# Causal self-attention scores of a transformer layer: three fp32r products of upper and lower halves in place of one fp32 product, and the output tile in another buffer's place

## What is computed

```python
    y = layernorm(x)                                   # (8, 512, 256)
    # attention(y, y, y, causal=True)
    scores = jnp.einsum('bqd,bkd->bqk', Q, K) / jnp.sqrt(d_k)
    scores = jnp.where(mask, scores, -inf)
    w = softmax(scores)
    sa = jnp.einsum('bqk,bkd->bqd', w, V)
    y = layernorm(y + sa)
```

## Time and profile before

| | |
|---|---|
| median of 3 runs | 622.27 us (617.64 to 622.56) |
| the profiled execution | 616.4 us, span 614.5 us |
| PE busy | 565.8 us, 92% of the span |
| DVE busy | 493.4 us, 80% |
| ACT busy | 378.4 us, 62% |
| POOL busy | 382.6 us, 62% |
| chain that ended last | PE 76%, issue 7%, POOL 6%, DVE 5%, ACT 4% |
| mean granted TensorE clock | 0.975 of full |

### The profile page before, as it was taken

The page is one execution under the profiler, slowest core; times in us unless marked ns, Lnnn a source line. Parts: engine busy times, 40 slices in busy tenths (PEclk is TensorE's granted clock), DMA queues, the critical chain, the costliest instruction groups (busy, mean ns, idle before and its releaser), DMA issues.

```text
span 614.5 us, 12404 instructions
## 1 busy us (share of the span) xinstructions
PE 565.8 (92%) x4021; PEld 537.4 (87%) x4021; DVE 493.4 (80%) x1220; ACT 378.4 (62%) x781; POOL 382.6 (62%) x466
## 2 busy tenths in 40 slices
PE   4776869999999999999999999999999999999765
PEld 3665868999999999999999999999999999989665
DVE  3688877888888888888888888887988878787762
ACT  3547465675748676667758575766666774746331
POOL 2554774676666766676657657675767656765621
PEclk9978979999999999999999999999999999999897
DMA  7700101010100101010101001010101010000000
GB/s 221 237 2 0 36 2 43 1 53 1 43 19 2 53 1 61 0 51 0 60 0 51 0 25 35 0 51 0 60 2 35 1 36 2 18 2 18 1 18 17
DMA packets 18742, 19.30 MB, mean 31 GB/s; under 512 B 1536, under 2 KB 18192, under 8 KB 18704
## 3 DMA queue, kind: packets, MB, share of 16 engines
q1 hardware_dynamic: 18704, 18.82, 10.0%
HBM read 14.62 MB, written 4.19 MB: 31 GB/s over the span
## 4 chain that ended last, share of the span: by engine, by line
PE 76%; issue 7%; POOL 6%; DVE 5%; ACT 4%; DMA 1%; SPq 1%; POOLq 0%; DVEq 0%; ACTq 0%
PE R L938 6%; PE R L940 5%; PE R L939 5%; PE TR L824 5%; PE O L986 5%; PE R L1004 4%; PE O L1049 4%; PE R L1006 4%; PE R L1005 4%; PE O L1051 4%; PE O L1050 4%; PE R L824 4%; PE O L1028 3%; PE O L1030 3%; PE O L1029 3%
## 5 line engine op out<-in xcount | busy, mean ns | idle before, releaser
L938 PE MATMUL R<-gu_hi,xqT_hi 128*128 128x352 f32 x256 | 85.4, 334 | 3.9 <-issue 3.0
L457 POOL TENSOR_TENSOR rs<-mv,neg_half 128x1 f32<-128x1 f32 (+1 forms) x112 | 69.2, 627 | 31.4 <-DVE mv L1277 30.1
L690 ACT ACTIVATE hqT_hi<-R 128x768 fp32r<-128x768 f32 x32 | 26.0, 813 | 98.8 <-PE R L824 98.8
L1004 PE MATMUL R<-y2T_hi,w_hi 128*128 128x256 f32 x256 | 77.3, 302 | 6.4 <-ACT e_full L717 3.4
L940 PE MATMUL R<-gu_hi,xqT_lo 128*128 128x352 f32 x256 | 82.4, 322 | 0.0
L939 PE MATMUL R<-gu_lo,xqT_hi 128*128 128x352 f32 x256 | 82.4, 322 | 0.0
L463 POOL TENSOR_TENSOR hs<-hh,h_rec 128x704 f32<-128x704 f32 x32 | 44.6, 1392 | 50.7 <-DVE h_rec L1313 50.7
L1049 PE MATMUL O<-w_hi,hT_hi 128*128 128x256 f32 x256 | 74.6, 291 | 0.0
L1006 PE MATMUL R<-y2T_hi,w_lo 128*128 128x256 f32 x256 | 73.1, 286 | 0.0
L1005 PE MATMUL R<-y2T_lo,w_hi 128*128 128x256 f32 x256 | 73.1, 285 | 0.0
L1051 PE MATMUL O<-w_hi,hT_lo 128*128 128x256 f32 x256 | 71.8, 281 | 0.0
(11 more groups left out here) (148 smaller groups left out, 1820.2 us busy)
## 6 DMA issues: line engine op xcount, KB each, us to landing
x_in<-in_x SPq DMA_DIRECT2D x16, 256.0 KB, 2.8
x_res<-in_x SPq DMA_DIRECT2D x16, 256.0 KB, 2.8
out<-x SPq DMA_DIRECT2D x32, 128.0 KB, 1.9
ctx_rows<-in_ctx SPq DMA_DIRECT2D x16, 64.0 KB, 2.5
hT<-in_L_xattn_w SPq DMA_DIRECT2D x1, 1024.0 KB, 8.0
hh<-in_L_xattn_w SPq DMA_DIRECT2D x1, 768.0 KB, 7.9
wd_raw<-in_L_ffn_w_down SPq DMA_DIRECT2D x1, 704.0 KB, 8.7
w_raw<-in_L_ffn_w_gate SPq DMA_DIRECT2D x1, 640.0 KB, 4.5
```

Source lines behind the costliest of these rows:

```text
L938: mm(o, xh, gu_hi[:, c, m, cols], start=(c == 0), stop=False)
L1004: mm(o, w1_hi[:, c, cols], y2T_hi[:, c, :], start=(c == 0), stop=False)
```

## The change

Three things change. `copy_y0T` on ACT writes the same copy as fp32r into `y0T_hi`. A new DVE instruction, `y0T_lower`, writes the bank minus `y0T_hi` into `y0T_lo`; it stands in DVE's slot after `hT_lower(b, g, 1)` and ahead of the place "self". Each fp32 product of the scores becomes three fp32r products, and the scores wait for `y0T_lo_set` as well as for `y0T_hi_set`. To make room, `x2` becomes numbers 512 to 1023 of each partition of `wd_raw`; its reads and writes stay as they were.

```diff
-        y0T = sb("y0T", [P, KC, S])
+        y0T_hi = sb("y0T_hi", [P, KC, S], F32R)
+        y0T_lo = sb("y0T_lo", [P, KC, S], F32R)
...
-        x2 = sb("x2", [P, T, D])
+        x2 = late_d(1)
...
-                act.activation(y0T[:, :, ROWS * h:ROWS * (h + 1)],
-                               TR[1][:].rearrange("p (c r) -> p c r", c=KC), ACT.Copy).then_inc(y0T_set, 1)
+                act.activation(y0T_hi[:, :, ROWS * h:ROWS * (h + 1)],
+                               TR[1][:].rearrange("p (c r) -> p c r", c=KC), ACT.Copy).then_inc(y0T_hi_set, 1)
...
+            def y0T_products(o, c, k, q, width):
+                keys, queries = slice(k, k + P), slice(q, q + width)
+                mm(o, y0T_hi[:, c, keys], y0T_hi[:, c, queries], start=(c == 0), stop=False)
+                mm(o, y0T_hi[:, c, keys], y0T_lo[:, c, queries], start=False, stop=False)
+                return mm(o, y0T_lo[:, c, keys], y0T_hi[:, c, queries], start=False, stop=(c == KC - 1))
+
             def scores(b, h):
-                wait(pe, y0T_set, b, h, 0, 1, 1)
+                wait(pe, y0T_hi_set, b, h, 0, 1, 1)
+                wait(pe, y0T_lo_set, b, h, 0, 1, 1)
...
-                    mm(bank(DIAG)[:, P:2 * P], y0T[:, c, q0 + P:q0 + ROWS], y0T[:, c, q0 + P:q0 + ROWS],
-                       start=(c == 0), stop=(c == KC - 1))
+                    y0T_products(bank(DIAG)[:, P:2 * P], c, q0 + P, q0 + P, P)
...
+            def y0T_lower(b, h):
+                wait(dve, y0T_hi_set, b, h, 0, 1, 1)
+                cols = slice(ROWS * h, ROWS * (h + 1))
+                v.tensor_tensor(y0T_lo[:, :, cols], TR[1][:].rearrange("p (c r) -> p c r", c=KC),
+                                f32(y0T_hi[:, :, cols]), ALU.subtract).then_inc(y0T_lo_set, 1)
...
                 if q1:
                     hT_lower(b, g, 1)
+                if live(b, h, 0):
+                    y0T_lower(b, h)
                 prepare(b, h, "self")
```

More of the change, by code:

```diff
@@ L211, in layer_program @@
         ln_out = [sem(f"ln_out{i}") for i in range(5)]
-        y0_turned, y0T_set = sem("y0_turned"), sem("y0T_set")
+        y0_turned, y0T_hi_set, y0T_lo_set = sem("y0_turned"), sem("y0T_hi_set"), sem("y0T_lo_set")
         scores_full, scores_diag = sem("scores_full"), sem("scores_diag")
@@ L955, in scores @@
                 for c in range(KC):
-                    mm(bank(DIAG)[:, P:2 * P], y0T[:, c, q0 + P:q0 + ROWS], y0T[:, c, q0 + P:q0 + ROWS],
-                       start=(c == 0), stop=(c == KC - 1))
+                    y0T_products(bank(DIAG)[:, P:2 * P], c, q0 + P, q0 + P, P)
                 for c in range(KC):
-                    last = mm(bank(DIAG)[:, 2 * P:4 * P], y0T[:, c, q0:q0 + P], y0T[:, c, q0:q0 + ROWS],
-                              start=(c == 0), stop=(c == KC - 1))
+                    last = y0T_products(bank(DIAG)[:, 2 * P:4 * P], c, q0, q0, ROWS)
                 last.then_inc(scores_diag, 1)
@@ L964, in scores @@
                         for c in range(KC):
-                            last = mm(bank(FULL)[:, ROWS * key:ROWS * (key + 1)], y0T[:, c, P * key:P * (key + 1)],
-                                      y0T[:, c, q0:q0 + ROWS], start=(c == 0), stop=(c == KC - 1))
+                            last = y0T_products(bank(FULL)[:, ROWS * key:ROWS * (key + 1)], c, P * key, q0, ROWS)
                     last.then_inc(scores_full, 1)
```

## The result

The changed kernel takes 627.65 us (median of 4 runs, 625.05 to 628.81) against 620.54 for the kernel before (median of 4, 617.64 to 622.56): a ratio of 1.0123, 95% interval 1.0079 to 1.0168, so some 7.6 us more (7.1 by the medians). That it is slower is clear of the noise; that it is slower by more than the 1% that the prediction named is not, since the interval begins at 0.79%. The profiled execution took 628.48 us, with a span of 626.5.

The account below looks back on a forecast made before the run. The prediction took PE to bound the steady part, with waits for other engines in slots 0 to 3. Steady +2.4 and start +4.4 gave +6.8 us, 629.1 on the 622.27 median; range 622 to 642 for 8 in 10.

Parts of the forecast that it names:

- the steady part: Slots 4 to 15: +0.30 us for each h = 0 slot, +0.10 for each h = 1, together +2.4 us.
- The price of a short fp32r product, p = 0.112: Scores on PE: a 128-column fp32r product takes 0.112 us, three 0.336 against 0.224 before; chance 0.42.
- The rival by fp32's price: Scores on PE: short fp32r products cost 0.224 us each; total +18.8 us, 641 us; chance 0.28.
- the one by columns: Scores on PE: short fp32r products cost 0.062 us each, by columns; total +1.6 us, 623.9 us; chance 0.12.
- The wait, 0.23 and 0.34: Steady slots: PE's first scores product ends later, waiting for DVE's lower part, by 0.23 us (h = 0) and 0.34 (h = 1).
- The products behind it, +0.07 and -0.24: Steady slots, scores after the first product: 1.27 us against 1.20 for h = 0, 2.68 against 2.93 for h = 1.
- What was costed at nothing: DVE's 0.68 us a slot, fitting into a 0.77 wait; the copy's new type; x2's home: no cost.
- The start, +4.4: Slots 0 to 3: DVE's order delays the scores; 3.2 + 1.0 + 0.2 = +4.4 us.
- Slot 0: Start: the lower part stands behind both find steps, so the scores end at 14.9 instead of 11.73: +3.2 us.
- the terms for slots 2 and 3: Start: slot 2 delays ff1 by 1.0 us, uncovered; slot 3 loses 0.2 us after cover.
- Slot 3's +0.2: Slot 3: scores end 2.8 us later, but PE's wait for e_full, with ACT behind, covers 2.6, leaving +0.2 us.
- The rival that the clock stays up in slot 3: Slot 3: PE's wait is cut in two, the clock doesn't fall, 2.3 us less; +4.5, 626.8 us; chance 0.10.

Follow-up runs that it names:

- e8: The changed kernel with each 128-wide product of the scores cut into two of 64 columns; one profile, span 638.3 us against the changed kernel's 626.5.
- e1: The changed kernel with its lower part and wait kept, but each scores product one fp32 product of the upper part; 1.0104 of the time before.
- e2: The changed kernel without the lower part and its wait, all three products upper part by upper part; 0.9927 of the time before.
- e5: The changed kernel with the first 6 of 18 products of down, tile 1, moved ahead of the scores on PE; 1.0039 of the time before.
- e7: e6 with the 128-wide scores product plain fp32 again from slot 4 on, from an added ACT copy; 1.0003 of the time before.
- e4: The kernel before with only x2 moved into the raw w_down's place; 0.9987 of the time before.
- e3: The changed kernel with the lower part at other places in DVE's order in slots 0 to 3; 1.0045 of the time before.
- e12: The changed kernel, unchanged, run once for a third profile; span 622.5 us.
- e10: The changed kernel, unchanged, run once for a second profile; span 627.6 us.
- e6: The changed kernel with both repairs, e3's DVE order in the first four slots and e5's split of down; 0.9994 of the time before.

## Why the prediction was right, point by point

The forecast was 629.1 us, or +6.8; the median is 627.65, and the ratio gives +7.6. The mean spans say the same: 617.5 for the four profiles of before's program and of x2's move, 625.5 for the three of the change, +8.0, made of +6.1 in the start, +3.2 in slots 4 to 15 and -1.2 in what follows, where the clock falls too at places that vary (the start and the tail thus carry a part that isn't the change's). The tail shows it: behind slot 15's scores, the profiles with 15 to 16 us at the lower level take 124.1 and 124.2 us in before's program, 123.8 to 124.3 in the change, and the two with 22 us take 126.5 and 126.4. So the forecast's sum came closer than its terms: the start was short by 1.7 and the steady part by 0.8, and the tail, for which no term stood, gave 1.2 back. That is luck.

- **The price of a short fp32r product, p = 0.112: right.** The change shows 0.11, e8 the floor itself. The rival by fp32's price (0.224) and the one by columns (0.062) both fall with it; they held 0.40 of the chance. On the Trainium skill's 81 ns ("TensorE: Matmul & The Clock Gate", "Back-to-back issue gap"): for fp32r the runs here don't agree with it, records of 64 and of 128 columns take 0.11 us; for other types no run here shows it.
- **The wait, 0.23 and 0.34: right. The products behind it, +0.07 and -0.24: a little too good.** In the prediction's own terms, the first product of the scores ends 0.33 us behind the record ahead for h = 0 and 0.41 to 0.47 for h = 1, in place of 0.11: 0.22 and 0.30 to 0.36 lost. What follows it takes 1.32 and 2.76 in place of 1.20 and 2.93: +0.12 and -0.17. The sum had left out that the first 256-wide record behind the short ones ends 0.17 after them, not 0.118, and the others take up to 0.120. (e1 and e2 share the step out otherwise, 0.27 and 0.37 to the wait, 0.07 and -0.22 to the products, because e2's first record ends 0.06 behind the one ahead; the totals are the same.) Twelve slots: 3.0 (steps) in place of 2.4.
- **What was costed at nothing:** DVE's 0.68 a slot was indeed covered in the change and in e5, whose 4 to 15 is that of e2 without the lower part (369.5 and 369.6). e7, with one more copy ahead of the lower part, shows how little of this cover is left. The home of x2 costs nothing that can be seen (e4). For DVE's 0.68 in each of the first four slots, where the weights are prepared, the sum had no term of its own, and no run takes it apart.
- **The start, +4.4: right in mechanism, too small.** Slot 0 went as forecast (its scores start at 11.99 and end at 14.89; predicted 12.0 and 14.9). Between the means of the three and the four profiles, the record ahead of slot 2's scores is 3.3 us later (51.1 against 47.8; predicted 3.2), that of slot 3's 5.1 (84.1 against 79.0; predicted 4.2) and that of slot 4's 6.1 (predicted 4.4). So the terms for slots 2 and 3, 1.0 and 0.2, came to 1.8 and 1.0. No term of the sum stood for the clock, and the clock was at its lower level for longer in two of the three profiles of the change. Whether that is the missing 1.7 stays open: the clock's places vary from execution to execution, but PE's new waits (3.95 us in slot 0, 2.9 in slot 3) may also move them, and seven profiles don't tell the two apart. e3 shows that the order on DVE causes 3.5 us.
- **Slot 3's +0.2 came about in another way than was said.** The cover, ACT's lateness, was measured at full clock. This is what follows in e12:

```profile
83.59 0.68 DVE L1416 TENSOR_TENSOR y0T_lo<-TR,y0T_hi 128x512 fp32r<-128x512 f32 x1
84.42 0.44 PE L953 MATMUL R<-y0T_hi 128*128 128x128 f32 x1 [2.86 <-DVE y0T_lo L1416]
84.66 0.41 PE L954 MATMUL R<-y0T_lo,y0T_hi 128*128 128x128 f32 x1
...
89.46 0.41 PE L955 MATMUL R<-y0T_hi,y0T_lo 128*128 128x256 f32 x1
89.91 0.69 ACT L718 ACTIVATE e_full<-R,neg_top 128x512 f32<-128x512 f32 x1 [1.98 <-PE R L955]
90.74 0.36 PE L1009 MATMUL R<-y2T_hi,w_hi 128*128 128x256 f32 x1 [0.87 <-ACT e_full L718]
```

The clock is at half speed through all 24 products of the scores (0.21 us each), which take 5.45 us (84.42 to 89.87) instead of the 3.05 of e10, where it is full (89.58 to 92.63), and ACT now waits 1.98 us for PE, where PE had waited for ACT. What that costs is given back in `ff1`, which now runs at full clock; in before it was the one at half speed. In the change's first profile it isn't given back, and the way from the record ahead of slot 3's scores to that of slot 4's takes 45.3 us in place of e12's 43.5 (43.2 in the first profile of before).

- **The rival that the clock stays up in slot 3:** it fell nonetheless in all three profiles, at 88.5, 102.0 and 83.5 us. In e10, where it fell last, slot 3's scores ran at full clock, so for that stretch the rival held in one of three.

## What to carry to other kernels

A product split into three parts needs its lower part, and here the wait for it, not the products, made the kernel slower: place that instruction by the time at which TensorE needs it in every slot, those of the start too, or put independent products in between (e5: six products hid it wholly). Then ask what is left to win: with both repairs this kernel was no faster than before (e6, 0.9994), since the 128-wide products lose most of what the 256-wide ones win. Count short products by number, not by columns: below some width they cost the same, so three fp32r products of 128 columns (0.34 us) are dearer than one of fp32 (0.22), and of 256 columns cheaper (0.36 against 0.43). And when TensorE gets faster by fractions of a microsecond a slot, look at the second busiest engine, and at what the change itself adds ahead of it, before counting the gain (e7).

## What the runs showed of the hardware that was not expected

Four profiles with the same instructions in the start reach slot 4 at 120.2, 121.2, 123.3 and 124.0 us, and three of the changed kernel at 125.0, 129.2 and 130.5. The four come in the order of the time for which the clock is at its lower level ahead of slot 4, the stretch up to its first rise included (41.3, 45.6, 46.8 and 50.8 us, as estimated above); that this makes the whole difference is not shown. The three of the change don't follow that order strictly (46.0, 64.6 and 61.0). In the steady part, where PE is busy for 436 of 440 us, the clock stays at full, and 4 to 15 repeats within 0.3 us. In a kernel like this one, a single profile of the start tells what a change is worth no closer than to 4 or 5 us. Also, a 64-column fp32r product takes what a 128-column one does, 0.112 us. And the clock's records leave out the time before its first rise, so the mean granted clock of a profile, 0.975 for before, is too high by that stretch.
